# The mix of a cross-attention block in two halves, with the logits columns behind them

## The chip, the core and the metric

The kernel runs on one core of one Trainium2 chip. The metric is the device time of one execution in microseconds (us). Five engines work side by side, each through its own list of instructions in order, and wait for one another by semaphores: TensorE (PE; its weight loads are shown apart as PEld), VectorE (DVE), ScalarE (ACT), GpSimd (POOL) and SyncE (SP), which here only issues transfers.

## What is computed

Two layers over `x` (2 x 2048 rows of 512), with a context of 2 x 128 rows. `_layernorm` has neither gain nor bias.

```python
x = x + xattn(_layernorm(x), ctx, ctx, mask)   # relu projections, no softmax
x = x + ffn(_layernorm(x))                     # x and weight quantised in blocks of 32
x = x + mix(_layernorm(x), ctx)                # "L1_xattn"
x = x + experts(_layernorm(x))                 # "L1_ffn"

def _L1_xattn_ref(x1, x2, W, b):
    W1, W2 = W[:, :d1], W[:, d1:]
    part1 = jnp.einsum('bld,ed->ble', x1, W1)
    part2 = jnp.einsum('bld,ed->be', x2, W2) / x2.shape[1]
    return part1 + part2[:, None, :] + b

def _L1_ffn_ref(x, Wg, bg, w1, b1, w2, b2, w3, b3):
    logits = jnp.einsum('bsd,de->bse', x, Wg) + bg       # 16 experts
    probs = jax.nn.softmax(logits, axis=-2)              # over the rows
    vals, idx = jax.lax.top_k(pv, K)                     # 128 rows for each expert
    ...                                                  # three layers, times vals, added to x
```

The change touches the mix and the logits that choose the rows of the experts.

## The kernel before

`N` is 32 tiles of 128 rows. Phase one takes the tiles through attention, ffn, mix and logits; phase two selects rows and runs the 16 experts. Products are made in three passes: each operand is split into a high part (`_h`, rounded, ScalarE) and a low part (`_l`, the rest, VectorE or GpSimd), and high x high, high x low and low x high are added in one PSUM bank. `three_passes` (L242) issues them, `four_transposes` (L249) turns a tile.

The order is written out by hand, engine by engine, as one loop over `k` with a pipeline of several tiles in flight. In iteration `k` TensorE does t3(k-2) (turns x2), ffn(k-1), t1(k+9) (turns a normalised x), in every fourth iteration scores, one `q_chunk`, t2(k) (turns xd), attend(k+1) and mix(k-2). VectorE does x1(k) and its sums, x3(k-3) (L1228, the result of the mix, which waits for the last matmul of mix(k-3)), the scales and q of the quantisation, the low parts, x2(k-1), and the sums of each norm. GpSimd makes the rstd (`rstd_of`, L1466 to L1475, three tiny operations a tile), xd, the additions of biases, and the low parts of q and of the scores (`q_lo`, `s_lo`, L1478). ScalarE makes the high parts (`hi`, L815), the relus of q (L863, L865) and, first in each iteration, `lt` (L919), the copy of the logits columns of tile k-3, which waits for `p_l`.

`mix(j)` multiplies x2T (four chunks d of 128 features) with the centred mix weights `wc_h`, `wc_l` (512 columns) into `ps_c` and with `wgs` into `ps_s`. `wgs` holds 64 columns a chunk: gate weights and mix weights times gate weights (2 x 16), high and then low. So the logits come from x2 without waiting for x3. `ps_s` is the bank of the scores too.

Before the loop stands the setup, interleaved with the first tiles: `norm1` and `t1` of tiles 0 to 9, keys, four chunks of q, `values`, `scores(0)`, the weights of ffn quantised (`wf scales`, `wf8`, L1113 to L1118) and turned (L588), the weights of mix summed (`wsum`, L1076), centred (`wcn`) and turned (`mix_weights`, L588), `mix_gate` (L624, mix weights times gate weights, unsplit float32 of 16 columns), and the mean of the contexts times W2 (`mean_columns`, L635, 16 products of 2 columns into four column blocks). Setup steps of the engines are called by name, `setup("wc0")` and so on, and order themselves by the lists A, V and T.

Of the kernel before, what the change touches and what calls it, by code (L numbers as in the profile page):

```python
# [26 lines left out]
F32 = mybir.dt.float32  # L27
# [7 lines left out]
P = 128  # L35
# [10 lines left out]
def build(nc, io):  # L46
# [20 lines left out]
        p_av p_t1 p_t2 p_t3 p_q p_f p_c p_s p_l p_seg  # L67
# [57 lines left out]
    wgs = place("wg_split", [P, C, 4 * E], F32R)  # L125
# [7 lines left out]
    at_wc = top[0]  # L133
    wc_h, wc_l = place("wc_h", [P, C, D], F32R), place("wc_l", [P, C, D], F32R)
# [38 lines left out]
    ctx_raw = place("ctx_raw", [P, C, CB], at=at_wc + 8 * KB)  # L173
    v32 = place("v32", [P, B, D], at=at_wc + 12 * KB)
    k32 = place("k32", [P, C, CB], at=at_ab + 4 * KB)
    wf8 = place("ffn_w_fp8", [P, C * D], FP8, at=at_ab)
    wstat = [place(f"ffn_w_stat{i}", [P, C * NB], at=at_seg + 256 * i) for i in range(3)]
    csum = place("ctx_sum", [P, C * B], at=at_seg + KB)
    cbcol = place("mix_bias_col", [P, C * B], at=at_seg + KB + 64)
    bccol = place("mix_b_col", [P, C], at=at_seg + KB + 128)  # L180
    w1mean = place("mix_w_mean", [P, C], at=at_seg + KB + 160)
# [33 lines left out]
    ps = banks(*[f"bank{i}" for i in range(8)])  # L215
    ps_ta, ps_tb, ps_q, ps_av, ps_f, ps_c, ps_s = ps[0], ps[1], ps[2:4], ps[4], ps[5], ps[6], ps[7]
    ps_wf = (ps_f, ps_c, ps_ta, ps_s)
    ps_wc = (ps_c, ps_s, ps_ta, ps_c)
# [63 lines left out]
    def q_units(k):  # L282

        if k < 3:
            return {1: [q_of(4), q_of(5)], 2: [q_of(7)]}.get(k, [])
        return [q_of(k + GRP + 1)] if k + GRP + 1 < N else []
# [22 lines left out]
    A = counts("wq0 wq1 k0 k1 k2 k3 v0 wf0 wf1 wf2 wf3 v1 wc0 wc1 wc2 wc3 row0 row1")  # L309
    V = counts("wgc wq0 wq1 mean wf8 wcn va0 v0 wf0 wf1 wf2 wf3 va1 wc0 wc1 wc2 v1 w1g wc3 cbcol cg")  # L310
    T = counts("wgm k0 k1 k2 k3 v0 wf0 wf1 wf2 wf3 v1 w1g wc0 wc1 wc2 wc3 col row0 cg row1")
# [17 lines left out]
    def phase1_over(eng):  # L329

        eng.wait_ge(sm.p_c, N)
        eng.wait_ge(sm.p_l, N)
# [111 lines left out]
    def _(pe):  # L444
# [24 lines left out]
        def t3(j):  # L469
            pe.wait_ge(sm.d_x2, j + 1)  # L470
            if j >= 1:
                pe.wait_ge(sm.d_lo3, j)
            else:
                pe.wait_ge(sm.d_set, V["wc2"])
# [6 lines left out]
        def q_chunk(g, c, n):  # L481
# [47 lines left out]
        def mix(j):  # L529
# [9 lines left out]
            def low(d):  # L539
                last = pe.matmul(ps_c[:, :], xl[:, d, :], wc_h[:, d, :], start=False, stop=False)  # L540
# [1111 lines left out]
```

## Time and profile before

| | us |
|---|---|
| median of 3 runs | 822.87 |
| lowest and highest | 822.21, 823.31 |
| the profiled execution | 825.72 |
| its span, first to last instruction | 823.2 |
| TensorE busy | 727.4 |
| VectorE busy | 573.3 |
| GpSimd busy | 439.6 |
| ScalarE busy | 372.4 |

The profile is one execution. Phase one ends at about 464 us; selection goes to about 515, the experts to the end. The ends of matmuls are modelled and overlap the next one, so the time of a matmul among others is read as the distance of two starts and not as its duration. A wait is written behind the row that ended it, with the instruction that released it.

### The profile page before, as it was taken

The numbers are of one execution on the slowest core, as the hardware profiler recorded it, in microseconds if no ns is written. First come the engines' busy times: TensorE is split into PE (matmuls) and PEld (weight loads), VectorE is DVE, ScalarE is ACT, GpSimd is POOL, SyncE is SP. The second block draws the span as 40 slices with busy tenths as digits, with TensorE's granted clock in tenths as the row PEclk, the third lists the DMA queues.
The fourth block names the chain that finished last, engine by engine and source line by source line (L and its number), as shares of the span: only waits on it lengthen the run. The fifth ranks groups of instructions, "written<-read, shape, count | busy, mean of one in ns | idle before, by whom it ended". The sixth has DMA issues, their size and how long they took to land.

```text
span 823.2 us, 12157 instructions
## 1 busy us (share of the span) xinstructions
PE 727.4 (88%) x4292; PEld 633.5 (77%) x4292; DVE 573.3 (70%) x1016; ACT 372.4 (45%) x540; POOL 439.6 (53%) x595
## 2 busy tenths in 40 slices
PE   6888999999999999999889200999999999999994
PEld 5666888888888888888677100899999999999993
DVE  5955478788787878777685698366667766666751
ACT  5634244444444444333222310366666566666540
POOL 2745578788778878777565250324333444333231
PEclk9999899999999999999999755899999999999998
DMA  9500012211221221111111504548887788887642
GB/s 313 204 14 27 25 65 78 79 65 65 79 78 66 77 79 52 52 54 52 40 52 54 199 7 159 154 141 233 243 243 216 228 245 238 239 239 240 185 89 39
DMA packets 54091, 103.02 MB, mean 125 GB/s; under 512 B 5392, under 2 KB 6672, under 8 KB 54032
## 3 DMA queue, kind: packets, MB, share of 16 engines
q1 hardware_dynamic: 46864, 85.47, 30.9%
q0 software_dynamic: 7168, 16.78, 9.1%
q8 instruction: 35, 0.57, 0.3%
q14 instruction: 24, 0.20, 0.1%
HBM read 76.68 MB, written 25.17 MB: 124 GB/s over the span
## 4 chain that ended last, share of the span: by engine, by line
PE 73%; DVE 14%; POOL 6%; DMA 2%; issue 2%; SPq 1%; ACT 1%; POOLq 0%; DVEq 0%; ACTq 0%
PE bank L242 51%; PE bank L249 5%; PE bank L549 5%; PE bank L547 5%; PE bank L540 4%; DVE pack L1310 1%; POOL xd L1539 1%; DVE left L1317 1%; DVE pos L1312 1%; DMA stage<-wq 1%; DVE x L1228 1%; POOL s_l L1478 1%; DVE bn L1046 1%; PE bank L448 1%; DVE q L1257 1%
## 5 line engine op out<-in xcount | busy, mean ns | idle before, releaser
L1578 POOL DMA_INDIRECT out<-y,ids x32 | 76.1, 2379 | 173.9 <-DVE y L1430 169.3
L1058 DVE TENSOR_TENSOR w_l<-w_raw,w_h 128x2048 fp32r<-128x2048 f32 x45 | 103.0, 2289 | 31.3 <-ACT w_h L815 30.2
L1046 DVE BATCH_NORM_STATS2 bn<-x 128x6 f32<-128x512 f32 x128 | 88.2, 689 | 8.0 <-DMA x<-x 4.7
L815 ACT ACTIVATE w_h<-w_raw 128x2048 fp32r<-128x2048 f32 x48 | 90.6, 1925 | 4.8 <-DMA w_raw<-w 4.8
L1009 ACT ACTIVATE h<-bank,b 128x512 f32<-128x512 f32 x64 | 44.0, 687 | 107.6 <-PE bank L242 107.6
L1058 DVE TENSOR_TENSOR hT_l<-h,hT_h 128x512 fp32r<-128x512 f32 x64 | 44.2, 691 | 67.1 <-ACT hT_h L1015 67.1
L1466 POOL TENSOR_SCALAR rstd<-mean_var 128x1 f32<-128x1 f32 x128 | 33.1, 259 | 95.5 <-DVE mean_var L1051 93.8
L242 PE MATMUL bank<-hT_h,w_h 128*128 128x256 f32 x256 | 72.4, 283 | 0.0
L242 PE MATMUL bank<-tokT_h,w_l 128*128 128x256 f32 x256 | 72.4, 283 | 0.0
L242 PE MATMUL bank<-hT_h,w_l 128*128 128x256 f32 x256 | 72.4, 283 | 0.0
L242 PE MATMUL bank<-tokT_l,w_h 128*128 128x256 f32 x256 | 72.4, 283 | 0.0
L242 PE MATMUL bank<-tokT_h,w_h 128*128 128x256 f32 x256 | 72.4, 283 | 0.0
L242 PE MATMUL bank<-hT_l,w_h 128*128 128x256 f32 x256 | 72.4, 283 | 0.0
L1567 POOL DMA_INDIRECT tok<-xn,ids x32 | 31.9, 997 | 47.7 <-DVE ids L1400 29.6
L242 PE MATMUL bank<-wf_h,xdT_h 128*128 128x512 f32 x128 | 53.7, 420 | 0.0
L1228 DVE SCALAR_TENSOR_TENSOR x<-bank,rstd_all,x 128x512 f32<-128x512 f32 x32 | 24.0, 751 | 39.8 <-PE bank L549 39.8
L242 PE MATMUL bank<-w_h,hT_h 128*128 128x512 f32 x128 | 51.3, 401 | 0.0
L242 PE MATMUL bank<-wf_h,xdT_l 128*128 128x512 f32 x128 | 51.3, 400 | 0.0
L242 PE MATMUL bank<-wf_l,xdT_h 128*128 128x512 f32 x128 | 51.2, 400 | 0.0
L242 PE MATMUL bank<-w_h,hT_l 128*128 128x512 f32 x128 | 50.0, 391 | 0.0
L242 PE MATMUL bank<-w_l,hT_h 128*128 128x512 f32 x128 | 49.8, 389 | 0.0
L242 PEld LDWEIGHTS bank<-hT_l,w_h 128*128 128x128 f32 x256 | 49.1, 192 | 0.6
(220 smaller groups left out, 2226.7 us busy)
## 6 DMA issues: line engine op xcount, KB each, us to landing
w_raw<-w SPq DMA_DIRECT2D x48, 1024.0 KB, 7.2
x<-x SPq DMA_DIRECT2D x32, 256.0 KB, 2.8
out<-x SPq DMA_DIRECT2D x32, 256.0 KB, 2.0
xn<-xn SPq DMA_DIRECT2D x32, 256.0 KB, 2.0
mask<-mask_t SPq DMA_DIRECT2D x8, 256.0 KB, 2.9
stage<-wk SPq DMA_DIRECT2D x1, 1024.0 KB, 9.7
stage<-wq SPq DMA_DIRECT2D x2, 512.0 KB, 9.3
stage<-wf SPq DMA_DIRECT2D x1, 1024.0 KB, 11.0
```

Source lines behind the costliest of these rows:

```text
L242: last = pe.matmul(out, a, b, start=(n == 0), stop=(n == 3 * len(pairs) - 1))
L249: last = pe.transpose(bank[:, c * P:(c + 1) * P], src[:, c * P:(c + 1) * P], ident[:, :])
L540: last = pe.matmul(ps_c[:, :], xl[:, d, :], wc_h[:, d, :], start=False, stop=False)
L547: pe.matmul(ps_c[:, :], xh[:, d, :], wc_h[:, d, :], start=(d == 0), stop=False)
L549: last = pe.matmul(ps_c[:, :], xh[:, d, :], wc_l[:, d, :], start=False, stop=(d == C - 1))
L815: act.activation(dst, src, ACT.Copy).then_inc(sem, 1)
L1009: act.activation(h32[n % 2][:, :], ps_hid[n % 4][:, :], ACT.Relu, bias=bias)
L1046: dve.bn_stats(bn6[which][:, j % 2, :], src[:, :]).then_inc(sem_bn[which], 1)
L1058: dve.tensor_tensor(dst, src, hi_part, ALU.subtract).then_inc(sem, 1)
L1228: dve.scalar_tensor_tensor(x3[j % 2][:, :], ps_c[:, :], r_all[0][:, j:j + 1], x2[j % 2][:, :], ALU.mult, ALU.add).then_inc(sm.d_x3, 1)
L1466: then(pool.tensor_scalar(r[:, 0:1], m[:, 1:2], LN_EPS, None, ALU.add))
L1578: pool.indirect_dma_start(out=out_rows, out_offset=bass.IndirectOffsetOnAxis(ap=ids[:, r:r + 1], axis=0), in_=y[e % 2][b][:, :], in_offset ...
```

## The change

One: `mix(j)` is issued in two halves of the 512 columns. Banks 6 and 7 are now one tensor, `both_halves`. `wc_h` holds, for each chunk and half, 256 mix columns and then 32 logits columns (high for half 0, low for half 1), 288 in all; `wgs` and the semaphore `p_l` are gone. x3 (VectorE) and `lt` (ScalarE) read both banks with one access, and `lt` waits for x3 and stands behind xc and x2T_h.

Two: the row sums of the mix weights and the centring move from VectorE (two passes of 2048 and a small one) to ScalarE, as four passes with a sum (`wsum`) and four with a bias (`wcn`).

Three: the rstd of tiles 4 to 9 is made for two tiles at a time.

Four: the setup is in another order. `scores(0)` stands ahead of t1(8); `mix_gate` is in one piece after two turned chunks; q(4) takes the place of `mix_gate` around t2(0); `wf8` is in four pieces, behind the statistics of tiles 6 to 9; the context sums move to the end of iteration 0; the mean of the contexts is made as rows (4 products of 512 columns), copied by ScalarE and turned to columns in the next iteration.

```diff
+    HALF = D // 2
+    WIDE = HALF + 2 * E
+    wc_h = place("wc_wg_h", [P, C, 2, WIDE], F32R)
...
     def mix(j):
...
+            def high(d):
+                for a in range(2):
+                    last = pe.matmul(both_halves[:, a, 0:WIDE], xh[:, d, :], wc_h[:, d, a, :],
+                                     start=(d == 0), stop=(d == C - 1))
                 return last
 
-            for d in range(C):
-                if d >= 1:
-                    low(d)
-                pe.matmul(ps_c[:, :], xh[:, d, :], wc_h[:, d, :], start=(d == 0), stop=False)
-                both = pe.matmul(ps_s[:, 0:4 * E], xh[:, d, :], wgs[:, d, :], start=(d == 0), stop=(d == C - 1))
-                last = pe.matmul(ps_c[:, :], xh[:, d, :], wc_l[:, d, :], start=False, stop=(d == C - 1))
-                if d == 0:
-                    low(d)
-            both.then_inc(sm.p_l, 1)
+            def low_weights(d):
+                for a in range(2):
+                    pe.matmul(both_halves[:, a, 0:HALF], xh[:, d, :], wc_l[:, d, a * HALF:(a + 1) * HALF],
+                              start=False, stop=False)
+
+            def low_tokens(d):
+                pe.matmul(both_halves[:, 0, 0:WIDE], xl[:, d, :], wc_h[:, d, 0, :], start=False, stop=False)
+                pe.matmul(both_halves[:, 1, 0:HALF], xl[:, d, :], wc_h[:, d, 1, 0:HALF], start=False, stop=False)
+
+            high(0)
+            low_weights(0)
+            low_tokens(0)
+            for d in range(1, C):
+                low_tokens(d)
+                low_weights(d)
+                last = high(d)
             last.then_inc(sm.p_c, 1)
...
+        def mean_rows():
+            for d in range(C):
+                last = pe.matmul(ps_s[0:B, :], csum[:, d * B:(d + 1) * B], stage[1][:, d, :],
+                                 start=(d == 0), stop=(d == C - 1))
...
+            if what == "wsum":
+                for c in range(C):
+                    last = act.activation(junk[:, c, :], stage[0][:, c, :], ACT.Copy, scale=-1.0 / D,
+                                          accum_out=w1mean[:, c:c + 1])
+            if what == "wcn":
+                for c in range(C):
+                    last = act.activation(stage[0][:, c, :], stage[0][:, c, :], ACT.Identity, bias=w1mean[:, c:c + 1],
+                                          scale=1.0)
...
-            j = k - 3
-            if valid(j):
-                act.wait_ge(sm.p_l, j + 1)
-                act.activation(lt[j // GRP % 2][:, j % GRP, :], ps_s[:, 0:4 * E], ACT.Copy).then_inc(sm.a_l, 1)
...
+            j = k - 3
+            if valid(j):
+                act.wait_ge(sm.d_x3, j + 1)
+                act.activation(four, both_halves[:, :, HALF:WIDE], ACT.Copy).then_inc(sm.a_l, 1)
...
+        def rstd1_pair(j):
+            pool.wait_ge(sm.d_st1, j + 2)
+            then(pool.tensor_scalar(r[:, :, 0], m[:, :, 1], LN_EPS, None, ALU.add))
+            then(pool.tensor_tensor(r[:, :, 1], r[:, :, 0], eps_exp[:, :].to_broadcast([P, 2]), ALU.pow))
+            then(pool.tensor_tensor(r[:, :, 2], m[:, :, 0], r[:, :, 1], ALU.mult))
+            pool.tensor_scalar(r[:, :, 2], r[:, :, 2], -1.0, None, ALU.mult).then_inc(sm.g_r1, 2)
```

On TensorE, the second half of a mix in phase one and what follows, before (`wg_split` is `wgs`):

```order
L540 MATMUL bank<-wc_h,x2T_0l 128x512
L541 MATMUL bank<-wg_split,x2T_0l 128x32
L547 MATMUL bank<-wc_h,x2T_0h 128x512
L548 MATMUL bank<-wg_split,x2T_0h 128x64
L549 MATMUL bank<-wc_l,x2T_0h 128x512
L249 MATMUL bank<-ident,x_1_126 128x128 x4
```

and now (`wc_wg_h` is `wc_h`):

```order
L565 MATMUL banks<-wc_wg_h,x2T_0l 128x288
L566 MATMUL banks<-wc_wg_h,x2T_0l 128x256
L561 MATMUL banks<-wc_l,x2T_0h 128x256 x2
L555 MATMUL banks<-wc_wg_h,x2T_0h 128x288 x2
L256 MATMUL bank<-ident,x_1_125 128x128 x4
```

Five matmuls of a chunk have become six, none under 256 columns.

On TensorE in the setup, from ffn(0)'s last matmul to the next q chunk, before (the first four transposes are t1(10)):

```order
L242 MATMUL bank<-wf_h,xdT_l 128x512
L249 MATMUL bank<-ident,xn_108 128x128 x4
L588 MATMUL bank<-ident,stage_145 128x128 x12
L242 MATMUL bank<-xT_1h,wq_h 128x512
L242 MATMUL bank<-xT_1l,wq_h 128x512
```

and now:

```order
L249 MATMUL bank<-wf_h,xdT_l 128x512
L256 MATMUL bank<-ident,xn_107 128x128 x4
L610 MATMUL banks<-ident,stage_144 128x128 x8
L645 MATMUL bank<-wg_pair,stage_144 128x16 x16
L249 MATMUL bank<-xT_1h,wq_h 128x512
```

Two of three turned chunks stay here, and all of `mix_gate` stands behind them.

On VectorE in the setup, from the scales of the ffn weights to the low part of `xT` of tile 6, before (`ffn_w_fp` is `wf8`, `bn` are sums):

```order
L1058 TENSOR_TENSOR xT_1l<-bank,xT_1h 128x4x128
L1046 BN_STATS bn_69<-x_104 128x6
L1051 BN_AGGR mean_var_65<-bn_69 128x2
L1118 TENSOR_TENSOR ffn_w_fp_152<-stage_148,ffn_w_stat_155 128x2048
L1058 TENSOR_TENSOR xT_1l<-bank,xT_1h 128x4x128
L1046 BN_STATS bn_69<-x_105 128x6
L1051 BN_AGGR mean_var_65<-bn_69 128x2
L1076 TENSOR_REDUCE mix_w_mean<-stage_145 128x4
L1077 TENSOR_SCALAR mix_w_mean<-mix_w_mean 128x4
L1058 TENSOR_TENSOR xT_1l<-bank,xT_1h 128x4x128
```

and now:

```order
L1096 BN_STATS bn_69<-x_103 128x6
L1101 BN_AGGR mean_var_65<-bn_69 128x2
L1096 BN_STATS bn_69<-x_104 128x6
L1101 BN_AGGR mean_var_65<-bn_69 128x2
L1108 TENSOR_TENSOR xT_1l<-bank,xT_1h 128x4x128
L1096 BN_STATS bn_69<-x_105 128x6
L1101 BN_AGGR mean_var_65<-bn_69 128x2
L1096 BN_STATS bn_69<-x_106 128x6
L1101 BN_AGGR mean_var_65<-bn_69 128x2
L1108 TENSOR_TENSOR xT_1l<-bank,xT_1h 128x4x128
L1165 TENSOR_TENSOR ffn_w_fp_151<-stage_147,ffn_w_stat_154 128x512 x4
```

The sums of tiles 6 to 9 have moved ahead of the long pass, which is in four pieces, and the mean of the mix weights is gone from VectorE.

## Rows read from the trace of the kernel before

**Rows 1.** The page, parts 1, 2 and 4: engines, granted clock, chain by engine.

```profile
PE 727.4 (88%) x4292; PEld 633.5 (77%) x4292; DVE 573.3 (70%) x1016; ACT 372.4 (45%) x540; POOL 439.6 (53%) x595
PEclk9999899999999999999999755899999999999998
PE 73%; DVE 14%; POOL 6%; DMA 2%; issue 2%; SPq 1%; ACT 1%; POOLq 0%; DVEq 0%; ACTq 0%
```

**Rows 2.** One stretch: us, busy us and count by engine, then granted clock, DMA.

```profile
148.00:196.00 48.00, 47.92 (x251) 39.92 (x250) 39.09 (x84) 21.84 (x39) 38.59 (x66) 1.00 0.22 74
```

**Rows 3.** Timeline, one chunk of mix: start us, duration us, engine, line, operation.

```profile
303.66 0.47 PE L547 MATMUL bank<-wc_h,x2T_1h 128*128 128x512 f32 x1
303.97 0.19 PE L548 MATMUL bank<-wg_split,x2T_1h 128*128 128x64 f32 x1
304.00 0.47 PE L549 MATMUL bank<-wc_l,x2T_1h 128*128 128x512 f32 x1
304.31 0.40 PE L540 MATMUL bank<-wc_h,x2T_1l 128*128 128x512 f32 x1
304.54 0.18 PE L541 MATMUL bank<-wg_split,x2T_1l 128*128 128x32 f32 x1
304.57 0.48 PE L547 MATMUL bank<-wc_h,x2T_1h 128*128 128x512 f32 x1
```

**Rows 4.** Timeline of TensorE in phase two, matmuls of 256 columns.

```profile
640.04 0.28 PE L242 MATMUL bank<-hT_h,w_h 128*128 128x256 f32 x1
...
640.16 0.28 PE L242 MATMUL bank<-hT_l,w_h 128*128 128x256 f32 x1
```

**Rows 5.** Timeline of VectorE in one ordinary stretch, with its two waits.

```profile
314.54 0.69 DVE L1058 TENSOR_TENSOR xdT_l<-bank,xdT_h 128x512 fp32r<-128x512 f32 x1 [0.90 <-ACT xdT_h L815]
...
317.55 0.75 DVE L1228 SCALAR_TENSOR_TENSOR x<-bank,rstd_all,x 128x512 f32<-128x512 f32 x1 [0.78 <-PE bank L549]
```

**Rows 6.** Timeline, the first load of attend after a scores stretch.

```profile
301.58 0.19 PEld L242 LDWEIGHTS bank<-v_h,s_h 128*128 128x128 f32 x1 [0.32 <-POOL s_l L1478]
```

**Rows 7.** Timeline of TensorE in the setup, waits in brackets.

```profile
31.77 0.66 PE L249 MATMUL bank<-ident,xn 128*128 128x128 f32 x4 [1.51 <-ACT xn L811]
...
35.99 3.60 PE L581 MATMUL bank<-stage,ctx_raw 128*128 128x512 f32 x8
40.44 0.66 PE L249 MATMUL bank<-ident,xn 128*128 128x128 f32 x4 [0.84 <-ACT xn L811]
43.86 0.50 PE L242 MATMUL bank<-qT_h,kT_h 128*128 128x512 f32 x1 [2.77 <-POOL qT_l L1478]
...
51.08 0.50 PE L242 MATMUL bank<-v_h,s_h 128*128 128x512 f32 x1 [0.85 <-DVE s_l L1058]
...
64.98 0.66 PE L249 MATMUL bank<-ident,xn 128*128 128x128 f32 x4 [1.43 <-ACT xn L811]
...
73.19 0.47 PE L242 MATMUL bank<-xT_1h,wq_h 128*128 128x512 f32 x1 [2.35 <-DVE wg_split L1058]
...
79.24 4.12 PE L635 MATMUL bank<-ctx_sum,stage 128*128 128x2 f32 x32
...
96.03 0.48 PE L547 MATMUL bank<-wc_h,x2T_0h 128*128 128x512 f32 x1
```

**Rows 8.** Three setup stretches, two at half clock; columns as in rows 2.

```profile
44.00:48.00 4.00, 4.00 (x11) 3.19 (x12) 0.00 (x0) 0.00 (x0) 3.41 (x1) 0.58 0.00 0
56.00:61.00 5.00, 4.96 (x41) 4.72 (x40) 4.13 (x9) 1.11 (x2) 2.45 (x3) 1.00 0.02 5
84.00:89.00 5.00, 5.00 (x14) 3.94 (x13) 1.64 (x4) 0.60 (x1) 2.31 (x3) 0.50 0.00 0
```

**Rows 9.** Timeline of VectorE and GpSimd in the setup.

```profile
27.46 2.26 DVE L1118 TENSOR_TENSOR ffn_w_fp<-stage,ffn_w_stat 128x2048 fp8e4<-128x2048 f32 x1
...
27.63 2.17 POOL L1466 TENSOR_SCALAR rstd<-mean_var 128x1 f32<-128x1 f32 x1 [2.73 <-DVE mean_var L1051]
```

**Rows 10.** Timeline of ScalarE, one pass of 128x512 from SBUF.

```profile
42.68 0.81 ACT L811 ACTIVATE xn<-x,rstd 128x512 f32<-128x512 f32 x1 [0.95 <-POOL rstd L1475]
```

More of the change, by code:

```diff
@@ L682, in _ @@
         values(0)
+        scores(0)
         t1(8)
-        scores(0)
         ffn_weights()
@@ L689, in _ @@
         attend(1)
-        mix_gate((0, 1))
+        q_chunk(*q_of(4), half=0)
         t2(0)
-        mix_gate((2, 3))
+        q_chunk(*q_of(4), half=1)
         for k in range(1, LAST + 1):
@@ L701, in _ @@
             if k == 1:
-                for kc in range(3):
-                    mix_weights(kc)
+                mix_weights(0)
+                mix_weights(1)
+                mix_gate()
+            if k == 2:
+                mean_columns()
             if scores_of(k) is not None:
@@ L901, in _ @@
         hi1(7)
+        setup("wsum")
         norm1(8)
         setup("v0")
+        s_relu(0)
         hi1(8)
         norm1(9)
-        s_relu(0)
         setup("wf0")
@@ L925, in _ @@
                     .then_inc(sm.a_xc, 1)
+            if k == 0:
+                setup("wcn")
             j = k - 2
@@ L961, in _ @@
             if k == 1:
+                setup("wc2")
+                setup("wc3")
                 q_relu(*q_units(k)[1])
-                setup("wc3")
-                q_relu(*q_of(6))
+                setup("crow")
             if k == 2:
@@ L1117, in setup @@
             if what == "wf8":
-                dve.tensor_tensor(wf8[:, :].rearrange("p (n k) -> p n k", k=QBLK), w, spread(rec, C * NB),
-                                  ALU.mult, saturate=False)\
-                    .then_inc(sm.d_set, 1)
+                for c in range(C):
+                    part = slice(c * NB, (c + 1) * NB)
+                    last = dve.tensor_tensor(wf8[:, c * D:(c + 1) * D].rearrange("p (n k) -> p n k", k=QBLK),
+                                             w[:, part, :], spread(rec[:, part], NB), ALU.mult, saturate=False)
+                last.then_inc(sm.d_set, 1)
             if what in ("wf0", "wf1", "wf2", "wf3"):
@@ L1167, in _ @@
         stats1(5)
-        setup("mean")
         setup("wf scales")
@@ L1186, in _ @@
         setup("wf0")
-        setup("wf1")
+        lo1(8)
         def logit_parts(g):
@@ L1236, in _ @@
             if k == 0:
-                lo1(9)
+                setup("wf1")
             if k == 1:
@@ L1262, in _ @@
                 setup("va1")
+                setup("mean")
             if k == 2:
@@ L1300, in _ @@
             if k == 1:
+                setup("wc2")
                 setup("wc3")
```

168 lines of the change are left out of this document (87 added, 81 removed).

## The prediction

> **What bounds the kernel now.** I read the page first: TensorE is busy 88% of the span, and the chain that ended last is 73% TensorE [rows 1]. A mean over stages decides nothing, so I next read the stretches. Phase one repeats every four tiles in 48.0 us; in such a stretch TensorE is busy 47.92 of 48.00 us at clock 1.00, VectorE 39.09, GpSimd 38.59, ScalarE 21.84 [rows 2]. TensorE sets the pace, with 8.9 us spare on the next engine. The reader should see that a microsecond taken from TensorE here comes off the span until another engine's chain is met; the waits say how near that is. In an ordinary stretch of one tile (11.2 us) VectorE waits twice: 0.90 us for `xdT_h`, 0.78 us for the end of mix [rows 5]. After a stretch with scores, TensorE itself waits 0.32 us for `s_l` [rows 6]. The setup (to the first mix at 96.03) is not bound so: TensorE waits 1.51, 0.84, 2.77, 0.85, 1.43 and 2.35 us there [rows 7], and twice works at half clock [rows 8]. Phase two is TensorE's too and is not touched.
>
> **Mix.** One chunk of mix today is five matmuls: three of 512 columns, one of 64, one of 32. From the start of L547 at 303.66 to its next at 304.57 it takes 0.91 us, so four chunks take 3.64 us [rows 3]. A 512-column matmul with another behind it takes 0.23 us (304.31 to 304.54) [rows 3]; three are 0.69, so the two small ones cost 0.22 us a chunk, 0.11 each, though they carry only 96 columns. The new chunk is six matmuls: three of 288 columns and three of 256. The column total is the same (1632), so this is no saving of arithmetic. In phase two, matmuls of 256 columns, each with a load of its own, start 0.12 us apart [rows 4]. For 288 columns no row exists. Bounds: 0.12 if the step is set by the load and not by columns; 0.12 x 288/256 = 0.135 if by columns alone. I take the upper, since 512 columns against 256 (0.23 against 0.12) goes nearly by columns. A chunk is then 3 x 0.12 + 3 x 0.135 = 0.765 us, a tile 3.06, against 3.64: **0.58 us less a tile**; by the lower bound 2.88, 0.76 less. The two PSUM banks alternate from matmul to matmul, but L547 and L548 already do that.
>
> The Trainium skill ("TensorE: Matmul & The Clock Gate", section "Back-to-back issue gap") gives N/2.4 + 2.5 ns from one matmul to the next. By that rule a chunk takes 0.70 us before and 0.70 us after, and the edit is worth nothing. The trace speaks against it: 0.91 us before, and 0.12 us instead of 0.109 for 256 columns.
>
> **Who follows mix.** Does VectorE keep up when mix ends 0.58 sooner? The work from mix's end through ffn, q and t2 is unchanged, so VectorE's step at 314.54 stays where it is relative to the last mix end, and only the 0.78 us wait before x3 shrinks, to 0.20 [rows 5]. No new wait. Even if VectorE became late at x3 by a tenth or two, TensorE would not feel it at once. The chain after a scores stretch (x3, q, xd, s_l) begins at x3 and moves with it, so the 0.32 us wait stays as it is and does not grow [rows 6]. The copy `lt` now waits for x3 and stands behind xc and x2T_h on ScalarE. Behind it wait hi1 (which waits far longer for t1 anyway) and, through `a_l`, scores and the next mix, over 3 us later. I cost it at nothing; the cover is ScalarE, busy 21.84 of 48 [rows 2]. x3 reads two banks by one access: same 512 elements, 0.75 us [rows 5], plus at most 0.1. In the tail without q the loop runs x3, xd, t2, attend, mix, x3, so mix is on it, and the 0.58 comes off too. 32 tiles: 18.6 us; with the lower bound 24.3.
>
> **Setup, stretch by stretch** (new starts are estimates from the order and the rows).
> To attend(0), 51.08 before: statistics of tiles 6 to 9 move ahead of the long VectorE passes. One of these, 2.26 us long, holds a tiny GpSimd operation for 2.17 us [rows 9]; it is now four pieces behind the statistics. The pair form needs both tiles' sums, and has four GpSimd instructions for two tiles in place of six. t1(6) waits about 0.4 in place of 1.51, and t1(7) loses its short wait: 1.7 with refilling. values(0) (about 3.45 us) starts at 35.99 now, 34.3 after, and ends where q_lo(3) is done (36.6); scores(0) follows at once, with t1(8) behind it, so the time from 39.4 to 43.86 goes but for the transposes: 4.0 us. Scores then runs at full clock: 44 to 48 at clock 0.58 is 3.4 us at half, 1.7 lost [rows 7, 8]. Sum 7.4; attend(0) near 43.7. Its own wait stays about 0.9: the same chain of s_relu, mask, s_l.
> To t1(10), 64.98 before: mix_gate (3.4 us) leaves and q(4) (2.8) enters, but ffn(0) now waits some 1.3 us for `xdT_l`, since the four centring passes on ScalarE (0.7 to 0.81 each [rows 10], some 3 us) and five more steps on VectorE stand ahead of it. 0.5 is given back: 58.1.
> To the mean of the contexts, 79.24 before: the 2.35 us wait for `wg_split` goes (2.6 with refilling), mix_gate in and q(4) out +0.6, a new wait for wc3 +0.7: 1.3 gained, start near 70.7.
> To the first mix, 96.03 before: 32 rows of L635 took 4.0 us; four matmuls of 512 columns (a row of L581 has the price, 3.60 with its tail) and four transposes take 3.8. The half clock that followed (84 to 89 at 0.50, 2.5 us lost [rows 8]) has no cause left, as wide matmuls stand there: 2.7 in all. First mix near **84.6, 11.4 us earlier**.
> Against this: from ffn(0)'s end there now stand a wait of 1.6 us, transposes and the whole of mix_gate in one piece, some 6 us without a wide matmul. Before, the clock was at half after a wait of 2.77 us and after 4 us of L635 [rows 7, 8]. I expect one fall here. The two seen cost 1.7 and 2.5 us; I take 1.9, since part lies on mix_gate, whose steps are not column-bound.
>
> **Sum.** 11.4 - 1.9 + 18.6 = 28.1 us. Span 823.2 to 795.1; the profiled execution, 825.72, to 797.6. The median of the runs is 822.87 and lies 0.3 below the span of the profiled one; I subtract from the median: **794.8 us**.
>
> **Rivals.**
> (a) The clock doesn't fall in mix_gate: 792.9. For: the stretch 56 to 61, mostly transposes and mix_gate, stayed at 1.00 [rows 8]. Chance 0.12.
> (b) 288 columns cost what 256 do: 5.7 more gained, 789.1. For: a load is the same for both. Chance 0.10.
> (c) The setup chain of waits is tighter than I make it, above all ffn(0) behind ScalarE's eight new passes and mean behind wc3: half of the 9.5 us comes, 799.6. Chance 0.18.
> (d) Another engine's chain takes over part of the mix gain. VectorE's spare falls from 8.9 in 48 to 6.6 in 45.7 us, and order makes part of it useless; if half of 18.6 is lost, 804.1. Against: the wait of 0.78 is longer than 0.58 [rows 5]. Chance 0.07.
> (e) A step set by each matmul and not by columns, as in the rule above but larger: at 3.64/24 = 0.152 us a matmul, mix is as long as before and only the setup's 9.5 is left: 813.4. Against: 0.12 in phase two [rows 4]. Chance 0.03.
> (f) The slower one: the same mechanism at the price of today's mix, 3.64/20 = 0.182 us for each load and matmul. 24 of them are 4.37 us, 0.73 more a tile, 23.3 in all, less 9.5: 836.7. It decides from 0.164 us a matmul, where the loss in mix equals those 9.5 us. Only if alternating banks at each step delayed the next matmul could this be. Chance 0.02.
> That the move of instructions is not as the code says is excluded by the order shown.
>
> **How the numbers follow.** The forecast has 0.48. (a), (b) and (c) with it are 0.88; with (d) 0.95. The range from 788 to 803 leaves out (e), (f), most of (d) and the outer part of the setup's uncertainty (3 us either way). About 0.2% is what a measurement of this kernel can tell from no change. All cases but (f) are faster; 0.96, same 0.01, slower 0.03.
>
> **What would show it.** In the changed profile: L555 to L566 start 0.12 to 0.135 us apart and a chunk is 0.77 (0.91 would be (e)); the four-tile period is 45.7 (over 47 would be (d)), with VectorE's wait before x3 at 0.2; the first mix at 84 to 87; no wait before scores(0); PE's clock below 1 once near 60, not at 45 and 85; phase two as long as before. A first mix later than 90, or a wait of TensorE on VectorE in each tile, would make the prediction wrong.

## The result

All times are medians of the device time; each ratio is against the kernel before in the same set of runs, with its 95% interval.

| kernel | us (lowest to highest) | ratio [95%] |
|---|---|---|
| before | 823.09 (822.21 to 823.61) | |
| after | 800.96 (799.52 to 801.92) | 0.9731 [0.9712, 0.9749] |

The change saves 22.1 us, 2.7%. The forecast was 794.8, a saving of 28.1, in a range of 788 to 803. The sign and the range held; 6 us of the gain are missing. The profiled span went from 823.2 to 799.9.

The page of the kernel after, the three lines that answer to [rows 1]:

```profile
PE 706.4 (88%) x4400; PEld 628.2 (79%) x4400; DVE 576.3 (72%) x1016; ACT 377.5 (47%) x553; POOL 432.3 (54%) x589
PEclk9998999999999999999999556999999999999998
PE 69%; DVE 16%; POOL 6%; issue 4%; DMA 2%; ACT 1%; SPq 1%; POOLq 0%; DVEq 0%; ACTq 0%
```

TensorE has 21.0 us less work and 108 matmuls more. VectorE is busy 3.0 us longer, though the change takes work from it: a first hint that something in it is held up by another engine.

One stretch of four tiles after, and the timeline of one chunk of mix; the numbers follow [rows 2] and [rows 3]:

```profile
136.30:182.35 46.05, 45.30 (x268) 39.53 (x267) 39.72 (x83) 21.90 (x38) 38.48 (x65) 1.00 0.24 76
```

```profile
194.26 0.29 PE L565 MATMUL banks<-wc_wg_h,x2T_1l 128*128 128x288 f32 x1
194.40 0.28 PE L566 MATMUL banks<-wc_wg_h,x2T_1l 128*128 128x256 f32 x1
194.51 0.40 PE L561 MATMUL banks<-wc_l,x2T_1h 128*128 128x256 f32 x2
194.75 0.43 PE L555 MATMUL banks<-wc_wg_h,x2T_1h 128*128 128x288 f32 x2
195.01 0.29 PE L565 MATMUL banks<-wc_wg_h,x2T_1l 128*128 128x288 f32 x1
```

A matmul of 288 columns steps 0.13 to 0.14 us, one of 256 steps 0.11 to 0.12, and the chunk from 194.26 to 195.01 takes 0.75 where the old one took 0.91. So four chunks are 3.0 us, and mix is 0.65 shorter. But four tiles are 46.05 us and not 48.0 less 4 x 0.65 = 45.4, and TensorE now idles 0.75 us in them, where it idled 0.08.

The starts of `x3`, one for each tile, show where. The distance from each to the next, in both traces:

| distances between `x3` | before, us | after, us | change |
|---|---|---|---|
| 22 without scores, the last two among them | 11.21, 10.73, 10.25; 8.21, 6.28 | 10.55, 10.07, 9.6; 7.56, 5.63 | -0.65 each |
| the first, with scores but without `lg_t` | 14.28 | 13.63 | -0.65; the 23 together -15.0 |
| 6 with scores and `lg_t`, and the one ahead of the third of them | 14.35 to 14.39 (five), 15.90; 11.22 | 14.33 to 14.37 (four), 14.01, 15.83; 10.95 | -0.8 in all |
| the one to tile 29, in the tail | 10.13 | 11.65 | +1.52 |
| `x3(0)` to `x3(31)` | 357.80 | 343.55 | -14.25 |

`lg_t` is the scaling of the logits of four tiles by VectorE (the function `logit_scale`). The first stretch with scores has none yet, and it gains the full 0.65.

Ahead of `x3(0)` 9.0 us went (99.97 to 90.98), behind `x3(31)` nothing (365.4 both times). 9.0 + 14.25 is the change of the span.

**The scores stretch.** VectorE and GpSimd just behind `x3`, of after and then of before:

```profile
182.35 0.75 DVE L1272 SCALAR_TENSOR_TENSOR x<-banks,rstd_all,x 128x512 f32<-128x512 f32 x1
...
183.57 1.29 POOL L1577 TENSOR_TENSOR x<-x,mix_bias 128x512 f32<-128x512 f32 x1
183.75 1.24 DVE L1250 TENSOR_TENSOR lg_t<-lg,rstd_all 128x64 f32<-128x64 f32 x1
184.86 0.67 DVE L1286 TENSOR_REDUCE amax<-xc 128x16 f32<-128x512 f32 x1
```

```profile
291.96 0.75 DVE L1228 SCALAR_TENSOR_TENSOR x<-bank,rstd_all,x 128x512 f32<-128x512 f32 x1 [0.67 <-PE bank L549]
...
292.55 1.29 POOL L1525 TENSOR_TENSOR x<-x,mix_bias 128x512 f32<-128x512 f32 x1
...
293.36 0.61 DVE L1207 TENSOR_TENSOR lg_t<-lg,rstd_all 128x64 f32<-128x64 f32 x1
293.84 0.67 DVE L1242 TENSOR_REDUCE amax<-xc 128x16 f32<-128x512 f32 x1
```

`lg_t` ends within 0.13 us of GpSimd's addition of the mix bias, and `amax` starts at the very time at which that addition ends (184.86; 293.84). `amax` is the head of the chain to `xd` and, in the orders of VectorE and GpSimd, to the mask of the scores and `s_l`. GpSimd's addition belongs to another tile and follows its statistics, which the end of mix doesn't move. It started 0.59 us behind `x3` before and starts 1.22 behind it now. So `x3` came 0.65 sooner and `amax` did not: it is 2.51 us behind `x3`, where it was 1.88. TensorE pays at the other end: it waits 0.76 where [rows 6] had 0.32, and attend starts 10.25 us behind `x3` (192.60) where it started 9.62 behind it (301.58 in [rows 6]). These 0.63 us take up what mix gives. The same timeline, TensorE:

```profile
192.60 0.50 PE L249 MATMUL bank<-v_h,s_h 128*128 128x512 f32 x1 [0.76 <-POOL s_l L1524]
```

**The tail.** TensorE in the stretch to tile 29 of after, then the clock of that stretch; then the same wait before:

```profile
415.98 0.66 PE L256 MATMUL bank<-ident,xd 128*128 128x128 f32 x4 [2.46 <-POOL xd L1591]
...
417.90 0.63 PE L561 MATMUL banks<-wc_l,x2T_1h 128*128 128x256 f32 x2
```

```profile
409.70:421.30 11.60, 9.14 (x50) 8.18 (x49) 7.34 (x14) 2.96 (x6) 6.95 (x12) 0.85 0.13 49
```

```profile
438.82 0.66 PE L249 MATMUL bank<-ident,xd 128*128 128x128 f32 x4 [1.82 <-POOL xd L1539]
```

The same held `lg_t` (1.23 us at 411.08; 0.60 before, at 434.55) makes the wait 2.46 us instead of 1.82. Behind it the clock falls to its lower level in the middle of mix (the two matmuls at 417.90 were followed by the next at 418.32, 0.42 us on, where 0.24 is usual, as at 194.51 above), and 1.5 us go; before, the clock stayed at 1.00 there. Whether the longer wait is what brought it down is looked at below.

**The setup.** TensorE with its waits, to be read beside [rows 7], and two stretches beside [rows 8]:

```profile
30.44 0.65 PE L256 MATMUL bank<-ident,xn 128*128 128x128 f32 x4 [0.84 <-ACT xn L840]
...
33.69 0.60 PE L256 MATMUL bank<-ident,xn 128*128 128x128 f32 x4
...
43.30 0.50 PE L249 MATMUL bank<-v_h,s_h 128*128 128x512 f32 x1 [0.37 <-DVE s_l L1108]
...
57.81 0.66 PE L256 MATMUL bank<-ident,xn 128*128 128x128 f32 x4 [1.60 <-ACT xn L840]
...
59.17 4.06 PE L645 MATMUL bank<-wg_pair,stage 128*128 128x16 f32 x32
...
73.55 3.59 PE L654 MATMUL banks<-stage,ctx_sum 128*2 128x512 f32 x8
...
87.71 0.51 PE L555 MATMUL banks<-wc_wg_h,x2T_0h 128*128 128x288 f32 x2
```

```profile
44.00:48.00 4.00, 3.67 (x13) 1.83 (x12) 3.64 (x8) 2.82 (x6) 1.24 (x4) 1.00 0.27 66
63.20:68.60 5.40, 5.40 (x15) 4.13 (x15) 2.77 (x8) 0.02 (x1) 3.45 (x6) 0.50 0.00 0
```

The row at 33.69 is t1(7). attend(0) stands at 43.30 (forecast 43.7), t1(10) at 57.81 (58.1), the full clock at 44 to 48 as foretold, and there is one fall, in the gate products, that lasts through the q chunk behind them. It costs more than forecast: the first mix is at 87.71, not at 84.6 + 1.9 = 86.5.

### The profile page after: what moved, and what is told of

The parts are those of the page before. It is cut to its first block, busy times and chain, and to the rows that moved or that the text cites. A ratio compares the mean times of both kernels' runs of the same rounds, so it can differ in the third digit from the quotient of the medians.

```text
span 799.9 us, 12388 instructions
## 1 busy us (share of the span) xinstructions
PE 706.4 (88%) x4400; PEld 628.2 (79%) x4400; DVE 576.3 (72%) x1016; ACT 377.5 (47%) x553; POOL 432.3 (54%) x589
## 4 chain that ended last, share of the span: by engine, by line
PE 69%; DVE 16%; POOL 6%; issue 4%; DMA 2%; ACT 1%; SPq 1%; POOLq 0%; DVEq 0%; ACTq 0%
PE bank L249 39%; PE banks L249 11%; PE bank L256 5%; PE banks L555 4%; PE banks L561 4%; DVE bn L1096 2%; PE banks L565 2%; PE banks L566 2%; DVE x L1272 1%; DVE pack L1356 1%; POOL xd L1591 1%; DVE left L1363 1%; DVE pos L1358 1%; DVE q L1301 1%; DMA stage<-wq 1%
## 5 line engine op out<-in xcount | busy, mean ns | idle before, releaser
L1512 POOL TENSOR_SCALAR rstd<-mean_var 128x1 f32<-128x1 f32 x122 | 29.4, 241 | 65.8 <-DVE mean_var L1101 62.6
L249 PE MATMUL banks<-w_h,hT_h 128*128 128x512 f32 x128 | 51.3, 401 | 0.0
L249 PE MATMUL banks<-w_h,hT_l 128*128 128x512 f32 x128 | 50.0, 391 | 0.0
L249 PE MATMUL banks<-w_l,hT_h 128*128 128x512 f32 x128 | 49.8, 389 | 0.0
L249 PEld LDWEIGHTS bank<-hT_h,w_h 128*128 128x128 f32 x256 | 49.1, 192 | 0.6
```

Source lines behind the costliest of these rows:

```text
L249: last = pe.matmul(out, a, b, start=(n == 0), stop=(n == 3 * len(pairs) - 1))
L1512: then(pool.tensor_scalar(r[:, 0:1], m[:, 1:2], LN_EPS, None, ALU.add))
```

## The experiments

The ratios are the measure of each kernel; their intervals reach 0.2 to 0.5% to either side, 1.5 to 4 us. A difference of one to three us between two changed kernels is thus read from their profiles, of which there is one for each, and is no more certain than that.

The first theory to test was **the held operation**: that the missing gain in mix comes from `lg_t`, which doesn't end before GpSimd's addition does. The rivals were that the new setup order shifted something in the loop, and that the mix itself gives less than its steps say.

### Each part alone

`mix_only` is the kernel before with the new mix; `setup_only` is the kernel after with the old mix and everything else new.

```diff
 mix_only, against before:
-    ps_wc ... wc_h, wgs; five matmuls a chunk (512, 64, 512, 512, 32 columns)
+    ps_cs = banks 6 and 7; wc_wg_h; six matmuls a chunk (288 and 256 columns); lt behind x3
 setup_only, against after: the same, the other way
```

> The kernel before with part one alone (mix in halves, lt behind x3), setup as before. If the two parts add up: mix is 0.65 us shorter in the 24 ordinary stretches and nothing shorter in the 8 stretches with scores or logits, one of which in the tail is even 1.5 us longer; so about 15 us faster than before, 808. If the scores stretches were spoilt by the new setup order and not by the mix, they are 0.65 shorter here too and the kernel takes about 803.

> The changed kernel with the mix, wgs, lt and x3 of before. If the parts add up, only the setup is earlier, by 99.97 - 90.98 - 0.65 = 8.3 us: about 815. The stretch after mix_gate is at half clock for some 5 us here as in the changed kernel. If the setup's gain needs the mix, less than 6 us is left.

Measured: `mix_only` 808.72 us (0.9824 [0.9789, 0.9860]), 14.4 less than before. `setup_only` 814.22 (0.9891 [0.9855, 0.9926]), 8.9 less. The sum, 23.3, agrees with the 22.1 of both together within the intervals: no sign that the parts disturb each other. In `mix_only` the `x3` distances are those of after: 10.55 without scores, 14.38 with them, and 11.68 in the tail. Only the last with scores is shorter (14.30 against 15.83), as the clock did not fall in it. VectorE and GpSimd in one of its scores stretches:

```profile
191.53 1.29 POOL L1540 TENSOR_TENSOR x<-x,mix_bias 128x512 f32<-128x512 f32 x1
```

```profile
191.70 1.25 DVE L1221 TENSOR_TENSOR lg_t<-lg,rstd_all 128x64 f32<-128x64 f32 x1
```

In `setup_only` `lg_t` takes 0.61, as before. The setup order is out as a cause; the new mix brings its loss with it.

### The scaling of the logits moved

```diff
-            if logits_of(k) is not None:
-                logit_scale(logits_of(k))
 (x3's steps: amax, xs, q, x2T_l, x2 ...)
             if g is not None:
                 s_mask(g)
+            if logits_of(k) is not None:
+                logit_scale(logits_of(k))
```

The same on the kernel after (`scale_late`) and on the kernel before (`before_scale_late`).

> The changed kernel with logit_scale (lg_t, L1250) moved on VectorE from behind x3's sums to behind the cast of s_h. Theory of the held operation: lg_t (1.24 us in the changed kernel, 0.61 before, ending both times when GpSimd's addition of mix_bias ends) lies in the chain x3, amax, q, xd, s_l, attend; away from there the scores stretch falls from 14.37 to about 13.7 us and TensorE's wait for s_l from 0.76 to 0; in the tail the wait for xd falls from 2.46 to about 1.3, and the clock doesn't fall behind it; in all 5 to 8 us faster than the changed kernel, 793 to 796. Rival, that s_l is late because of GpSimd's own row of work (xd, additions, rstd): under 1 us, and the wait for s_l stays at 0.7.

> The kernel before with the same move of logit_scale (L1207). There lg_t costs 0.48 us of the chain, but TensorE waits only 0.32 for s_l, so the theory of the held operation gives 8 times 0.3 and 0.5 in the tail: 2 to 3 us faster than before, about 820.5. Rival (GpSimd's own row): no change.

Measured: `scale_late` 796.94 us (0.9673 [0.9639, 0.9707]), 4.0 below after. VectorE and GpSimd of it where `lg_t` stood, and where it stands now:

```profile
182.28 0.75 DVE L1272 SCALAR_TENSOR_TENSOR x<-banks,rstd_all,x 128x512 f32<-128x512 f32 x1
...
183.50 1.29 POOL L1577 TENSOR_TENSOR x<-x,mix_bias 128x512 f32<-128x512 f32 x1
183.68 0.67 DVE L1284 TENSOR_REDUCE amax<-xc 128x16 f32<-128x512 f32 x1
...
190.34 0.27 DVE L1250 TENSOR_TENSOR lg_t<-lg,rstd_all 128x64 f32<-128x64 f32 x1
...
411.94 0.81 DVE L1250 TENSOR_TENSOR lg_t<-lg,rstd_all 128x64 f32<-128x64 f32 x1
```

`amax` starts 1.40 us behind `x3`, no more 2.51, and runs beside the addition. TensorE's wait of 0.76 for `s_l` is gone. The scores stretch takes 13.68 us, 0.69 less than after: the gain of mix that had been missing. The tail stretch takes 10.25 instead of 11.65, with a wait of 1.57 for `xd` and the clock at 1.00. By the `x3` distances 5.7 us were won, 4.2 in the stretches with scores and 1.4 in the tail; 1.0 was lost again elsewhere in the span (0.6 ahead of `x3(0)`, the rest behind `x3(31)`). The 4.0 us are less than the 5 to 8 expected. One reason is in the last row: in the tail the moved `lg_t` meets another GpSimd addition, takes 0.81, and TensorE waits 0.70 us for it.

`before_scale_late` came out at 825.1 with a ratio of 0.9998 [0.9964, 1.0031]: no change that can be measured, though its profiled span is 3.4 shorter. Its scores stretches of 14.38 us stayed as they were; only the last two got shorter (14.35 to 13.91 and 15.90 to 13.88, the second mainly because the clock did not fall in it), and a tail stretch got longer (10.13 to 10.68). The 2 to 3 us expected did not come. The mask of the scores shows why, before and then with the move:

```profile
202.94 0.69 DVE L1143 TENSOR_TENSOR s<-s,mask 128x512 f32<-128x512 f32 x1 [0.20 <-ACT s L871]
```

```profile
201.60 0.69 DVE L1143 TENSOR_TENSOR s<-s,mask 128x512 f32<-128x512 f32 x1 [0.53 <-ACT s L871]
```

VectorE waited for `s` from ScalarE in both, so what the move freed went into that wait, and TensorE's load waited 0.32 us for `s_l` as before. In after the mask has no such wait. So the position cost the old kernel next to nothing, and became a cost with the faster mix.

### What holds the operation

```diff
-            dve.tensor_tensor(lg_t, lg[:, :, :], r_all[1][:, four] (broadcast), ALU.mult)
+            dve.tensor_copy(lg_t, lg[:, :, :])
```

> The changed kernel with the logits copied in place of scaled: the same 128x64 elements by VectorE in the same place and behind the same waits, but with one operand in SBUF where there were two. Left out: the scaling by rstd. Theory 1 (VectorE's operation with two operands in SBUF can't run beside GpSimd's addition of the mix bias, L1577, and is held to its end): a copy isn't held, takes about 0.3 us and not 1.24, the scores stretch is 13.7 us and not 14.37 and the time that of the kernel with the scaling moved, 796.9. Theory 2 (anything that VectorE starts there is held or waits for what GpSimd writes): 1.2 us for the copy and 801.0.

Measured: 799.66 us (0.9718 [0.9694, 0.9742]), with scores stretches of 14.30 to 14.36 (13.98 and 15.78 where after has 14.01 and 15.83). GpSimd and VectorE of this kernel:

```profile
182.05 1.30 POOL L1576 TENSOR_TENSOR x<-x,mix_bias 128x512 f32<-128x512 f32 x1
182.23 1.20 DVE L1250 COPY lg_t<-lg 128x64 f32<-128x64 f32 x1
```

My theory of two operands fell: a copy with one operand is held just as long. The 1.3 us below after come from the setup (`x3(0)` at 89.46), not from here. But not everything is held: in `scale_late` the reduction `amax` ran its usual 0.67 beside the same addition. The small `xs` behind it (128x16, one tensor operand) took 0.44 instead of 0.23, and ended with the addition too. The Trainium skill ("SBUF — State Buffer", section "SBUF: two separate sides") says that VectorE and GpSimd have one pair of ports in common, an exclusive lock for the whole of an instruction, which VectorE wants for an operation with two operands in SBUF or in a 2-port mode, and a note in that section counts a float32 copy within SBUF among the latter. By that rule both forms are held and the reduction isn't; the three rows agree. Whether the ports are the mechanism no run here shows. That most of the 1.24 us is waiting and not work is shown by the price of `lg_t` elsewhere, 0.27.

### The clock in the setup

The second theory: the half clock at 61 to 70 us, worth more than the 1.9 of the forecast, needs both the wait of 1.60 and the small matmuls behind it. `q5_early` puts tile 5's q chunk into the wait. `q5_split` leaves the wait and puts half of the chunk between the transposes and the gate products.

```diff
 q5_early                                  q5_split
+  q_chunk(q_of(5))                           t1(10); mix_weights(0); mix_weights(1)
   t1(10); mix_weights(0); mix_weights(1)  +  q_chunk(q_of(5), half=0)
   mix_gate()                                 mix_gate()
-  q_chunk(q_of(5))                        +  q_chunk(q_of(5), half=1)
```

> The changed kernel with one instruction group moved: tile 5's q chunk (12 matmuls of 512 columns) is issued ahead of t1(10) and the gate products, where it came behind them. Theory 1 (the fall of the clock in the setup is paid for, and is brought on by the 1.60 us wait ahead of t1(10) together with the small matmuls behind it): the q chunk fills the wait and the clock stays at 1.00 at 56 to 72 us; the clock part is worth about 2.6 us (the q chunk took 5.31 us at half clock where 2.7 is its full-clock time) and the filled wait up to 1.6 more, so 796.8 us with all of it, 798.4 with the clock alone, against 801.0. Theory 2 (the small matmuls of the gate bring the clock down by themselves, whatever stands ahead): 799.4 (the wait alone) and 0.5 clock behind the gate again. Theory 3 (the start of phase two hangs on another engine's work on the weights, not on TensorE): 801.0, with a longer wait further on.

> The changed kernel with the same work in that place, but the q chunk in two halves, one between t1(10) and the gate products and one behind them. The wait of 1.60 us ahead of t1(10) is left as it is. Theory 1 (the wait and the small matmuls in a row bring the clock down): the first half of wide matmuls parts them, the clock stays at 1.00 and the time is 798.4 us, 2.6 below 801.0. Theory 2 (the gate products alone bring it down): the second half runs at half clock, 1.3 us lost rather than 2.6, 799.7. Theory 3 (the wait alone brings it down): the fall comes about as early, and the time is 801.0 or above.

Measured: `q5_early` 798.79 us (0.9690 [0.9643, 0.9736]), `q5_split` 797.88 (0.9684 [0.9638, 0.9730]). The windows of `q5_early`, then of `q5_split`:

```profile
56.00:61.00 5.00, 5.00 (x37) 4.52 (x35) 2.94 (x7) 3.49 (x7) 2.26 (x6) 1.00 0.00 0
61.00:68.00 7.00, 7.00 (x37) 6.60 (x37) 5.16 (x12) 3.16 (x7) 4.59 (x8) 0.58 0.00 1
```

```profile
56.00:61.00 5.00, 3.42 (x26) 3.12 (x25) 2.63 (x7) 4.09 (x7) 2.25 (x7) 1.00 0.00 0
61.00:68.00 7.00, 7.00 (x52) 6.41 (x52) 5.42 (x13) 2.47 (x5) 4.90 (x8) 1.00 0.00 1
```

With the wait filled, TensorE was busy all the time and the clock fell all the same: the wait is not needed for it. `q5_early` still has `x3(0)` 2.3 us earlier (88.72), for the filled wait. With wide matmuls between the transposes and the gate products the clock stayed up, here behind a wait and in `late_split_warm` below without one; the gate products alone did not bring it down. `x3(0)` is at 87.66 in `q5_split`, 3.3 us earlier, which is about the fall's price: in `setup_only`, which has the order of after, the clock stayed at 1.00 in its profile, and there the way from t1(10) to the mean of the contexts is 57.17 to 69.75, 12.58 us; after needs 57.81 to 73.55, 15.74. Difference 3.2; `q5_split` needs 12.59. The rows of `setup_only`, the gate products and the mean of the contexts:

```profile
58.54 3.64 PE L633 MATMUL bank<-wg_pair,stage 128*128 128x16 f32 x32
...
69.75 3.60 PE L642 MATMUL bank<-stage,ctx_sum 128*2 128x512 f32 x8
```

The fall is thus not certain in that order: eight profiles with the transposes directly ahead of the gate products had it at 60 to 70 us, `setup_only` did not; and in the four kernels with the setup of after unchanged (after, `scale_late`, `tail_warm`, `logits_copied`) it put `x3(0)` anywhere from 89.46 to 91.59. `mix_only`, with the old order of the setup, had a clock of 0.50 at 61 to 64 us where before had 1.00. What decides it in these I can't say, and that parting the small matmuls keeps the clock up rests on two profiles.

### The clock in the tail

```diff
-                keep_warm(3 if valid(k) else 6, wq_h, ps_q[0])
+                keep_warm(7 if valid(k) else 6, wq_h, ps_q[0])
```

> The changed kernel with 7 instead of 3 filling matmuls in each tile of the tail (four more at 0.23 us each in waits of 1.36, 1.36, 1.35 and 2.46 us for xd, and in one of 3.18 us for s_l). They lie within the waits and so cost nothing. If the fall of the clock at 416 to 421 us (0.85 in 409.7 to 421.3, the mix at half clock from 417.4) comes from the wait of 2.46 us, it stays at 1.00 and the stretch that took 11.65 us takes about 10.15: 799.5 us against 801.0. If not, 801.0 and the same stretch.

Measured: 800.23 us (0.9704 [0.9657, 0.9751]); the difference to after is within the spread. The stretch itself is plain: 10.10 us instead of 11.65, `x3(0)` to `x3(31)` 1.5 shorter, and the window of it at full clock:

```profile
409.70:421.30 11.60, 10.03 (x62) 8.73 (x61) 8.79 (x17) 3.69 (x8) 7.81 (x13) 1.00 0.14 50
```

That looks as if the wait of 2.46 us were the cause. Two other kernels speak against so simple a rule. `q5_split`, in which nothing of the tail was touched, has the same wait and no fall (10.11 us; these 1.5 us are in its profile beside those of the setup), and `late_and_early`, further down, has a wait of 1.56 and the fall (11.76). The two in this order:

```profile
412.78 0.66 PE L256 MATMUL bank<-ident,xd 128*128 128x128 f32 x4 [2.47 <-POOL xd L1595]
```

```profile
406.47:416.58 10.11, 7.64 (x50) 6.68 (x49) 7.36 (x14) 2.97 (x6) 6.95 (x12) 1.00 0.15 56
```

```profile
406.09 0.66 PE L256 MATMUL bank<-ident,xd 128*128 128x128 f32 x4 [1.56 <-POOL xd L1594]
```

```profile
400.70:412.46 11.76, 9.50 (x50) 8.22 (x49) 7.17 (x14) 3.09 (x6) 6.79 (x12) 0.85 0.13 48
```

Of the 14 profiles, seven have a wait of 2.45 to 2.50 us, and six of these the fall; seven have one of 1.82 or less, and one of these. So the long wait makes the fall likely and doesn't decide it, and what does stays open.

### Two steps of the setup undone

`t1_first` has the old order of t1(8) and scores(0) on TensorE; `rstd_single` computes the rstd of tiles 4 to 9 one by one.

```diff
 t1_first                 rstd_single
         values(0)        -        rstd1_pair(4)
-        scores(0)        +        rstd1(4)
         t1(8)            +        rstd1(5)
+        scores(0)         (6 and 8 likewise)
```

> The changed kernel with the old order of t1(8) and scores(0) on TensorE. The transposes of tile 8 need xn, which ScalarE has at 38.79 us; values(0) ends at 37.7. Theory (this order is part of the setup's gain): TensorE waits some 1.1 us ahead of t1(8), which with the transposes puts scores(0) 1.6 us later; attend(0) is as much later, at 44.9, and the time 802.6. If the wait also brings the half clock of the kernel before back to scores(0), 1.7 more: 804.3. Rival (attend(0) hangs on ScalarE and VectorE and not on the scores): 801.0.

> The changed kernel with rstd of tiles 4 to 9 computed one tile at a time on GpSimd again (24 small operations in place of 12; a pair took about 1.65 us from first to last, a single one no less than 1.4 by the three operations in their place, as the power alone is 0.72 for two). Theory (the pairs are what shortened the wait ahead of t1(6) to 0.84): 6 to 8 comes up to 1.4 us later each, the waits ahead of t1(6) and t1(7) grow by about 1 us in all and the time is 802. Rival (the order of the statistics did it, and the pairs cost as much by waiting for the second tile as they save): 801.0, or below it by up to 0.7.

Measured: `t1_first` 802.18 us (0.9752 [0.9724, 0.9780]), `rstd_single` 799.66 (0.9721 [0.9697, 0.9746]). TensorE in `t1_first`, t1(7), t1(8) and attend(0):

```profile
34.71 0.60 PE L256 MATMUL bank<-ident,xn 128*128 128x128 f32 x4
...
39.86 0.66 PE L256 MATMUL bank<-ident,xn 128*128 128x128 f32 x4 [1.11 <-ACT xn L840]
...
45.86 0.50 PE L249 MATMUL bank<-v_h,s_h 128*128 128x512 f32 x1 [0.86 <-DVE s_l L1108]
```

And attend(0) in `rstd_single`:

```profile
42.71 0.50 PE L249 MATMUL bank<-v_h,s_h 128*128 128x512 f32 x1 [0.37 <-DVE s_l L1108]
```

attend(0) is 2.56 us later (45.86 against 43.30), but t1(7), ahead of which the two kernels have the same order, is already 1.02 later (34.71 against 33.69). The order is worth the other 1.5, the 1.6 that was expected; about 1 is left at `x3(0)`. The wait of 1.11 did not bring the clock down as one of 2.77 had before. The pairs are worth nothing: without them t1(6) doesn't wait at all (29.12 against 30.44), scores(0) waits 0.41 for `qT_l` instead, and attend(0) comes 0.6 earlier, about as much as the profiles of the unchanged order differ among themselves (43.30 to 43.91). The first tile of a pair has to wait for the statistics of the second; that this is the reason is argued, not shown.

### All of it together

`late_and_early` joins `scale_late` and `q5_early`. `late_split_warm` joins `scale_late`, the q chunk of tile 5 in two halves (one in the wait ahead of t1(10), one between the transposes and the gate products) and the filling of the tail.

> Both orders changed: VectorE's scaling of the logits behind the masked scores, and tile 5's q chunk ahead of t1(10) and the gate products. If the two losses are separate, as their places say (one from 97 to 440 us, one ahead of 73 us), the gains add: 796.9 less 2.6 to 4.2, so 792.7 to 794.3 us. If the setup's gain is given back before the first mix, 796.9.

> What helped, together: the scaling of the logits behind the masked scores; the first half of tile 5's q chunk in the 1.6 us wait ahead of t1(10) and the second half between the transposes and the gate products; 7 filling matmuls in each tile of the tail. Against 796.9 us of the first alone: the wait filled (1.35 us of half a q chunk in 1.59) and the clock not falling (2.6 to 2.9): 792.8 us. The tail's filling is worth nothing if the clock stays up there as it did with the first alone, 1.5 if it falls as it did in the kernel with both orders (a tail stretch of 11.76 us against 10.25). If the clock falls in the setup all the same, 795.6.

Measured: 794.47 us (0.9646 [0.9599, 0.9693]) and **792.71 us (790.98 to 793.40), 0.9637 [0.9613, 0.9662]**. The second is the fastest kernel of the study, 8 us below after. TensorE at t1(10) and at the mean of the contexts in it:

```profile
57.59 0.66 PE L256 MATMUL bank<-ident,xn 128*128 128x128 f32 x4 [0.23 <-ACT xn L844]
...
70.08 2.31 PE L654 MATMUL banks<-stage,ctx_sum 128*2 128x512 f32 x5 [1.26 <-DVE wc_l L1112]
```

The clock stayed up, in the setup (1.00 at 61 to 68 us) and in the tail. But the filled wait brought nothing: the 1.37 us that t1(10) waits less come back as 1.26 us ahead of the mean of the contexts, for `wc3` from VectorE, and `x3(0)` is at 87.51, where `q5_split` had it at 87.66. What took its place in the profile's sum I had not reckoned with, and it may be luck: in the last scores stretch the clock falls and 1.5 us go in before, after and `scale_late` (15.90, 15.83, 15.08 us), and not in the two combined kernels (13.53 and 13.54), nor in `mix_only` and `before_scale_late` (14.30, 13.88). Against after, then, the profile of `late_split_warm` has 3.5 from the setup and 7.2 from there to `x3(31)`, 5.7 of it the logits with the tail's fall. The expected 792.8 was met, but not by the terms it was made of. `late_and_early` had a clock fall in the tail (11.76 us); `late_split_warm`, with the filling, takes 10.24.

## Why the prediction was right, and where it was off

- **What bounds the kernel**: right. TensorE set the pace, and a shorter mix came off the span in each tile without scores.
- **The price of mix**: right, and the gain a little low. A chunk is 0.75 us, not 0.765; a tile gains 0.65, not 0.58. By columns was the right reading; the per-matmul rivals (e) and (f) fell, and (b) with them: 288 columns cost more than 256. The formula of the Trainium skill named there would have given no gain; the mix alone gave 14.4 us. The same section ("TensorE: Matmul & The Clock Gate", "Back-to-back issue gap") says that the formula is for an isolated matmul, counts too little at few columns, as the loads are left out, and too much at 512 (it gives 131 ns as measured). With the first the trace agrees (0.11 us for 32 and 64 columns), with the second not (0.23 us for 512).
- **"No new wait", and "begins at `x3` and moves with it, so the 0.32 us wait stays as it is"**: this step failed. The wait grew to 0.76. The chain moves with `x3` only where nothing that hangs on another engine stands in it; `lg_t` does, and hangs on GpSimd. Nor was the 0.32 set by this chain alone: taking 0.48 us out of it in `before_scale_late` left the 0.32 as it was. Had the chain moved with `x3`, 31 distances would have given 31 x 0.65 = 20.2; they gave 14.25. The scores stretches lack 7 x 0.65 - 0.8 = 3.8, the tail 1.52 + 0.65 = 2.2. `scale_late` brings 4.2 back in the scores stretches, all that was lacking there, and 1.4 in the tail. Rival (d) named the right kind of loss (half of mix gain lost, 804.1); 5.9 of 20.2, about 30%, was lost. I had looked at VectorE's waits in a stretch without scores [rows 5] and at the end of the chain in one with scores [rows 6], never at what stands between. [rows 9] showed the very effect, a GpSimd operation of 2.17 us held by VectorE's, and I used it in the setup only.
- **The tail**: "mix is on it, and the 0.58 comes off too" held for each tile but one, where the clock fell. That term was not in the sum. In the two kernels with `lg_t` held there and the clock up (`tail_warm`, `q5_split`) the stretch takes 10.1 us, as before, so the held `lg_t` costs the 0.65 of mix and the clock the 1.5.
- **The setup**: right in place, by 0.4 us at attend(0) and t1(10), though not by its reasons. Its terms, 7.4 - 0.5 + 1.3 + 2.7, add up to 10.9, where the forecast has 11.4; with the fall's 3.2 given back the profile has 11.5, so that the slip happened to help. The pair form, to which the shorter wait of t1(6) was put down, is worth nothing (`rstd_single`). The order of t1(8) and scores(0) had 4.0 + 1.7 us to its name; undoing it costs 1.5 at attend(0), and no half clock. The rest was the order of statistics and long passes, which I didn't take apart.
- **The clock fall in the gate products**: foreseen, at 1.9 us; it costs 3.2. Its cause was put down to "a wait of 1.6 us, transposes and the whole of mix_gate"; the wait is not needed for it (`q5_early`).
- **The sum**: forecast 9.5 + 18.6 = 28.1. In the profile 8.3 to the first mix, 0.65 for tile 0's mix and 14.25 behind it, 23.2 of a span that is 23.3 shorter; in the medians 22.1. So of the 6 us that are missing, 3.7 are mix (14.9 for 18.6), 1.2 the setup with its fall, and the rest is what the two profiled executions and the medians differ by. That the forecast came this near is in part luck: the held `lg_t` and the tail's fall took 5.9 us, and the better price of a chunk gave back 2.2. (The last chances give slower 0.03, though only (f), 0.02, is slower.) Phase two was untouched, as said.

## What to carry to other kernels

When an engine on the path gets faster, don't ask only whether the next engine has a wait to spare; list, for each kind of stretch, what stands in the consumer's queue between the moved event and the end of the chain, and on what each of these hangs. A small operation ahead of a chain is free only while nothing holds it: put what isn't urgent behind the chain, and look at what it meets there. And fill or part a run of small matmuls with wide ones that have to be done anyway; that was worth 3 us in the setup here, in the two kernels that did it, for no work.

## What the runs showed of the hardware

- A VectorE operation of 0.27 us (128x64, within SBUF) took 1.24 beside a GpSimd addition of 1.29, and ended with it; so did a copy, 1.20. A reduction of 128x512 kept its 0.67; a scaling of 128x16 with one tensor operand took 0.44 instead of 0.23.
- It seems to work both ways: in `scale_late` GpSimd's power of 128x1, usually 0.57 us, took 1.19 when it began together with VectorE's mask of 128x512.
- The clock fell in a stretch in which TensorE was busy throughout (`q5_early`, 5.00 of 5.00 us and then 7.00 of 7.00 at 0.58), when transposes and 32 matmuls of 16 columns stood in a row; it did so in eight of nine profiles with these in a row, and in none of the two in which six wide ones parted them.
- In the tail it fell in six of the seven profiles with an idle time of 2.45 to 2.50 us, and in one of the seven with 1.82 or less.
- A matmul with a load of its own among others steps 0.23 us for 512 columns, 0.13 to 0.14 for 288, 0.11 to 0.12 for 256, and still 0.11 for 64 or 32.
